# Block-diagonal copies of turned q and k by DMA instead of by three engines, and k turned ahead of q

## The reference

```python
# block 1, for each of 16 batches: N = 128 positions, C = 128, H = 16 heads, HD = 8
mod = silu(c) @ ada_w.T + ada_b                      # shift, scale, gate for both halves
h = layernorm(x) * (1 + scale_msa) + shift_msa
q, k, v = split(h @ qkv_w.T + qkv_b)                 # each 16 heads x 128 x 8
attn = einsum('bhnd,bhmd->bhnm', q, k) * HD ** -0.5
attn = softmax(where(mask, attn, -1e9))
x = x + gate_msa * (einsum('bhnm,bhmd->bhnd', attn, v) @ proj_w.T + proj_b)
x = x + gate_mlp * (gelu(mod(layernorm(x)) @ fc1_w.T + fc1_b) @ fc2_w.T + fc2_b)
```

## Time and profile before

| | |
|---|---|
| time, three runs | 249.68, 250.20, 250.73 us; median 250.2 us |
| span of the profiled execution | 249.0 us (its own device time is not listed apart; the span lies 1.2 us below the median of the runs) |
| busy over the whole span | PE 206.9 us, DVE 186.8, ACT 180.2, POOL 163.5 |
| the 16 steps | about 72.5 to 213 us of the span |
| granted TensorE clock | full in nearly all slices |

### The profile page before, as it was taken

The page is one execution under the profiler, slowest core; times in us unless marked ns, Lnnn a source line. Parts: engine busy times, 40 slices in busy tenths (PEclk is TensorE's granted clock), DMA queues, the critical chain, the costliest instruction groups (busy, mean ns, idle before and its releaser), DMA issues.

```text
span 249.0 us, 5248 instructions
## 1 busy us (share of the span) xinstructions
PE 206.9 (83%) x1596; PEld 154.1 (62%) x1596; DVE 186.8 (75%) x530; ACT 180.2 (72%) x381; POOL 163.5 (66%) x287
## 2 busy tenths in 40 slices
PE   0689998999998687977978787897888778998894
PEld 0548875678876466755746655665666556564784
DVE  0673895647199998989989989989998999058514
ACT  2147769545758788997998988989899877984330
POOL 2499589998676586875876776677689723338500
PEclk9999999999999999999999999999999999999999
DMA  6950000071000000000000000000000000000112
GB/s 159 413 219 0 4 1 0 5 295 42 0 4 0 0 3 1 4 1 0 0 0 0 0 0 0 0 0 0 0 0 3 0 0 3 0 3 0 42 42 86
DMA packets 2768, 8.28 MB, mean 33 GB/s; under 512 B 496, under 2 KB 832, under 8 KB 2496
## 3 DMA queue, kind: packets, MB, share of 16 engines
q1 hardware_dynamic: 2176, 6.22, 6.7%
q10 hardware_dynamic: 576, 1.86, 2.0%
HBM read 7.01 MB, written 1.06 MB: 32 GB/s over the span
## 4 chain that ended last, share of the span: by engine, by line
DVE 34%; PE 31%; issue 19%; ACT 6%; POOL 5%; DMA 2%; DVEq 1%; POOLq 0%; ACTq 0%
PE ps L305 8%; DVE nmax L938 7%; PE ps L295 7%; DVE kdiag L933 7%; DVE nmdiag L956 5%; PE ps L253 3%; DVE xn L781 3%; PE ps L353 2%; PE ps L241 2%; DMA xs<-x 2%; DVE nm L946 2%; PE ps L364 2%; DVE bn_c L979 2%; POOL rstd L1080 2%; DVE qk L923 2%
## 5 line engine op out<-in xcount | busy, mean ns | idle before, releaser
L665 ACT ACTIVATE qdiag<-qxT 32x512 fp32r<-32x512 f32 x64 | 40.2, 628 | 1.4
L938 DVE TENSOR_REDUCE nmax<-ps 128x8 f32<-128x1024 f32 x32 | 37.7, 1217 | 2.2 <-PE ps L353 1.6
L670 ACT ACTIVATE shared<-ps 128x1024 f32<-128x1024 f32 x32 | 31.0, 1021 | 6.6 <-PE ps L377 6.6
L353 PE MATMUL ps<-kdiag,qxT 128*128 128x512 f32 x64 | 20.5, 436 | 16.2 <-DVE kdiag L933 16.2
L1209 POOL TENSOR_TENSOR qkx<-qk,qkx 128x256 fp32r<-128x256 f32 x32 | 22.8, 734 | 16.3 <-ACT qkx L650 16.2
L1214 POOL TENSOR_TENSOR kdiag<-kxT,quarter 128x512 fp32r<-128x512 f32 x16 | 19.9, 1244 | 19.4 <-ACT kxT L659 19.4
L621 ACT ACTIVATE hid<-ps,W 128x512 f32<-128x512 f32 x32 | 21.6, 691 | 14.7 <-PE ps L295 14.6
L933 DVE CAST kdiag<-kxT 32x512 fp32r<-32x512 f32 x48 | 31.2, 651 | 1.0 <-ACT kxT L659 0.6
L305 PE MATMUL ps<-W,hid 128*128 128x128 f32 x256 | 29.9, 275 | 0.0
L305 PEld LDWEIGHTS ps<-W,hid 128*128 128x128 f32 x256 | 29.4, 192 | 0.6 <-issue 0.5
L295 PE MATMUL ps<-hT,W 128*128 128x512 f32 x64 | 29.4, 598 | 0.0
(11 more groups left out here) (148 smaller groups left out, 477.8 us busy)
## 6 DMA issues: line engine op xcount, KB each, us to landing
gate<-gates SPq DMA_DIRECT2D x1, 2048.0 KB, 6.9
xs<-x SPq DMA_DIRECT2D x4, 256.0 KB, 9.4
mask_i<-mask ACTq DMA_DIRECT2D x1, 1024.0 KB, 9.5
W<-weights SPq DMA_DIRECT2D x1, 768.0 KB, 12.0
out<-xs SPq DMA_DIRECT2D x3, 256.0 KB, 2.3
R<-rows ACTq DMA_DIRECT2D x1, 512.0 KB, 7.0
W<-weights SPq DMA_DIRECT2D x1, 512.0 KB, 10.8
W<-weights SPq DMA_DIRECT2D x1, 392.0 KB, 10.1
```

What stands on the lines that cost most here:

```text
L353: ins = mm(ps[:, t, :], qxT[u][:, t], kdiag[u][:, t], start=True, stop=True)
L665: ins = a(qdiag[u][rows, :, r], qxT[u][rows], ACT.Copy)
L670: a(pT[u][:, 2 * e:2 * e + 2], ps[:, 2 * e:2 * e + 2, :].rearrange("n t (r q) -> n t r q", r=4), ACT.Exp, scale=HD ** -0.5).then_inc(s["c_ ...
L938: v.tensor_reduce(nmax[u][:, 8 * e:8 * e + 8], ps[:, 2 * e:2 * e + 2, :].rearrange("n t (r k) -> n (t r) k", r=4), AX.X, ALU.max, negate=T ...
```

## The change

`kdiag` and `qdiag` are filled by DMA. SP, idle before, runs over the 16 batches: it waits until `kxT` of the batch is there, issues four transfers of 32 partitions x 2 KB (64 KB each, on-chip source and destination), waits until `qxT` is there, and issues four more. The semaphores `c_kd` and `c_qd` now count 16 for each transfer, and PE waits for all four. The layout of both tiles becomes (r, t, N) in place of (t, r, N), so that a transfer writes 2 KB in one piece in each partition, and the matmuls read four pieces of 128 columns instead of one of 512. The copies on ACT, DVE and POOL, the tile `quarter` and the semaphore `c_kd3` are gone. k now comes ahead of q everywhere: in DVE's `front_qk`, ACT's `front_hi`, POOL's `lower`, and in PE's and ACT's lists, where `front_k` takes the early place and `front_q` the late one. `front_k` keeps its waits for `c_turn` and `c_v`.

```diff
+            def spread(to, of, b, signal):
+                for r in range(4):
+                    rows = slice(32 * r, 32 * r + 32)
+                    sp.dma_start(to[b % 2][rows, r].bitcast(F32), of[b % 2][rows].bitcast(F32)).then_inc(s[signal], 16)
+
+            sp.wait_ge(s["diag_ok"], 4)
+            for b in range(B):
+                sp.wait_ge(s["c_kT"], b + 1)
+                if b > 1:
+                    sp.wait_ge(s["c_S"], 2 * b - 2)
+                spread(kdiag, kxT, b, "c_kd")
+                sp.wait_ge(s["c_qT"], b + 1)
+                if b > 1:
+                    sp.wait_ge(s["c_ST"], 2 * b - 2)
+                spread(qdiag, qxT, b, "c_qd")
...
             def front_q(b, u):
-                pe.wait_ge(s["c_lo"], 2 * b + 1)
+                pe.wait_ge(s["c_lo"], 2 * b + 2)
...
             def front_k(b, u):
-                pe.wait_ge(s["c_lo"], 2 * b + 2)
+                pe.wait_ge(s["c_lo"], 2 * b + 1)
                 pe.wait_ge(s["c_turn"], b + 1)
                 pe.wait_ge(s["c_v"], b + 1)
...
                     pe.wait_ge(s["c_qT"], b + 1)
-                    pe.wait_ge(s["c_kd"], b + 1)
-                    pe.wait_ge(s["c_kd3"], b + 1)
+                    pe.wait_ge(s["c_kd"], 64 * b + 64)
...
-                    ins = mm(ps[:, t, :], qxT[u][:, t], kdiag[u][:, t], start=True, stop=True)
+                    ins = mm(bank(t), qxT[u][:, t], kdiag[u][:, :, t], start=True, stop=True)
...
-                    pe.wait_ge(s["c_qd"], 3 * b + 3)
+                    pe.wait_ge(s["c_qd"], 64 * b + 64)
...
-                    mm(ps[:, t, :], kxT[u][:, t], qdiag[u][:, t], start=True, stop=False, skip_group_check=True)
+                    mm(bank(t), kxT[u][:, t], qdiag[u][:, :, t], start=True, stop=False, skip_group_check=True)
... PE's step
                 if front:
-                    front_q(b + 1, 1 - u)
+                    front_k(b + 1, 1 - u)
...
                 if front:
-                    pe.wait_ge(s["c_k"], b + 2)
+                    pe.wait_ge(s["c_q"], b + 2)
                 turn_maxima(b, u)
                 scores_t(b, u, 1)
                 if front:
-                    front_k(b + 1, 1 - u)
+                    front_q(b + 1, 1 - u)
... ACT's step
-                front_qdiag(b, u, (1, 2))
                 if end:
                     projected(b - 2, u)
-                front_qdiag(b, u, (3,))
                 if back:
                     back_o(b - 1, 1 - u)
                 if front:
                     front_v(b + 1, 1 - u)
+                    front_k(b + 1, 1 - u)
                     front_q(b + 1, 1 - u)
-                    front_qdiag(b + 1, 1 - u, (0,))
-                    front_k(b + 1, 1 - u)
... DVE's and POOL's steps
-                if front:
-                    front_kdiag(b + 1, 1 - u)
```

More of the change, by code:

```diff
@@ L119, in build @@
         row_mask = sb("row_mask", [128, 1])
-        quarter = sb("quarter", [128, 1])
         row_amp = sb("row_amp", [128, 1])
@@ L186, in build @@
             b_pow b_xn b_xb b_T b_h b_M1 b_gelu b_M2 b_res
-            c_pow c_xb c_gp c_nv c_qbv c_xc c_Tx c_h c_QK c_V c_q c_k c_v c_hiq c_hik c_lo c_Tq c_Tk c_qT c_kT c_qd c_kd c_kd3
+            c_pow c_xb c_gp c_nv c_qbv c_xc c_Tx c_h c_QK c_V c_q c_k c_v c_hiq c_hik c_lo c_Tq c_Tk c_qT c_kT c_qd c_kd
             c_S c_max c_nm c_NT c_nmT c_ST c_exp c_PV c_oT c_T2 c_rden c_on c_T3 c_onT c_pr c_at c_ga c_res c_st
@@ L521, in _ @@
             pe.wait_ge(s["c_h"], 2)
+            pe.wait_ge(s["c_q"], 1)
+            front_k(0, 0)
             front_q(0, 0)
-            front_k(0, 0)
-            pe.wait_ge(s["c_k"], 1)
             front_b(1, 1)
@@ L646, in front_hi @@
             def front_hi(b, u):
-                for n, (ready, slots, signal) in enumerate((("c_q", slice(0, 2), "c_hiq"), ("c_k", slice(0, 4, 2), "c_hik"))):
+                for n, ready, slots, signal in ((1, "c_k", slice(0, 4, 2), "c_hik"), (0, "c_q", slice(0, 2), "c_hiq")):
                     act.wait_ge(s[ready], b + 1)
@@ L659, in front_k @@
                 a(kxT[u][:], bank(7), ACT.Copy).then_inc(s["c_kT"], 1)
[L661 to L666, removed]
             def weights_of(b, u, e):
@@ L716, in _ @@
             a(spare[:], spare[:], ACT.Exp)
+            front_k(0, 0)
             front_q(0, 0)
-            front_k(0, 0)
-            act.wait_ge(s["diag_ok"], 4)
-            front_qdiag(0, 0, (0,))
             step(0, 0, end=False, back=False)
@@ L810, in _ @@
             v.tensor_reduce(sel_f[:], mod32[:, 0:8].rearrange("p (k t) -> p t k", t=4), AX.X, ALU.add)
-            v.tensor_reduce(quarter[:], ident[:, 96:128], AX.X, ALU.add)
             v.tensor_reduce(row_mask[:], mod32[:, MROW:32], AX.X, ALU.add).then_inc(s["mod32_ok"], 1)
@@ L922, in front_qk @@
                 dve.wait_ge(s["c_qbv"], b + 1)
+                v.tensor_tensor(qk[u][:, 1].rearrange("n h d -> n (h d)"), ps[:, 4, C:2 * C], row("qk_b", C, C), ALU.add)\
+                    .then_inc(s["c_k"], 1)
                 v.scalar_tensor_tensor(out=qk[u][:, 0].rearrange("n h d -> n (h d)"), in0=ps[:, 4, 0:C],
@@ L925, in front_qk @@
                     .then_inc(s["c_q"], 1)
[L926 to L934, removed]
             def maxima(b, u, e):
@@ L1026, in _ @@
             front_qk(0, 0)
-            dve.wait_ge(s["diag_ok"], 4)
             b_residual(2)
-            front_kdiag(0, 0)
             front_qk(1, 1)
@@ L1168, in _, with prepare @@
                 p.memset(m[:].bitcast(F32), 0.0).then_inc(s["diag_ok"], 1)
-            def prepare(b, u, end=False, last_kdiag=False):
+            def prepare(b, u, end=False):
                 settled(pool)
@@ L1196, in prepare @@
                 p.tensor_tensor(turn_k[u][:], keep[u][:], one, ALU.add).then_inc(s["c_turn"], 1)
-                if last_kdiag:
-                    front_kdiag(b - 1, 1 - u)
                 if not isinstance(b, int) or b >= 2:
@@ L1204, in lower @@
             def lower(b, u):
-                for n, (hi, lo, signal) in enumerate(((slice(0, 2), slice(2, 4), "c_hiq"),
-                                                      (slice(0, 4, 2), slice(1, 4, 2), "c_hik"))):
+                for n, hi, lo, signal in ((1, slice(0, 4, 2), slice(1, 4, 2), "c_hik"),
+                                          (0, slice(0, 2), slice(2, 4), "c_hiq")):
                     pool.wait_ge(s[signal], b + 1)
@@ L1210, in lower @@
                                     qkx[u][:, n, :, hi], ALU.subtract).then_inc(s["c_lo"], 1)
[L1212 to L1215, removed]
             def residual_1(b, u):
@@ L1232, in step @@
                 if ahead:
-                    prepare(b + 2, u, end, True)
+                    prepare(b + 2, u, end)
                 else:
```

## The result

The changed kernel takes 253.9 us in the median of five runs (253.09 to 259.26), against 250.27 for the kernel before; the ratio is 1.0139 with a 95% interval of 1.0112 to 1.0166. It is slower, by 3.6 us. The likeliest case of the prediction (no change) did not come; its first rival did, the chain through the DMA, near the D of 3.9 for which it gave a period of 9.1 and 255 us. The measured time lies inside the stated range (248 to 260), but in the part that stood there for this rival. A second set of runs of the same kernel gave 253.84 us and 1.0165 (1.0111 to 1.0219).

What follows compares the result with a forecast made beforehand. DVE was taken as the bound before, the loop through ACT and PE after. 13 periods +0.65, step 1 -0.6, jumps +0.75, end -0.6: +0.2 on span 249.0; median 1.2 above: 250.4 us, range 248 to 260.

Steps and rivals of the forecast that it cites:

- The likeliest case of the prediction: Whole kernel: period 8.82 us a step against 8.77, so about no change, 250.4 us; chance 0.43.
- first rival: PE's wait for `c_kd` before the scores becomes the bound from D = 3.6; 255 to 265 us; chance 0.31.
- D: Four `kdiag` issues plus landing of the last: taken as 1.41 + 1.9 = 3.3 us, other side 4.6.
- What bounds the kernel before: DVE runs almost without a gap; PE waits for its `kdiag` copies before the scores, 13.4 us in all.
- What is removed: Per step about 2.0 us of copies on DVE and 2.5 on ACT, leaving 6.3 and 5.4; neither full.
- Loop two: Dependences through the `kdiag` DMA to the next scores: period 5.21 + D, 8.5 us, hidden by 0.3.
- Loop one: Dependences through ACT and PE, from one step's second exponential to the next: 8.79 us, taken as 8.82.
- `qdiag` costed at nothing: `qdiag` transfers on SP land before PE needs them in the next step, with 2.8 us of cover.
- The strided operand at nothing: Matmuls reading four pieces of 128 columns cost nothing, with up to 0.1 us per step as other bound.
- Transfers one after the other: Rival at the four transfers: they serialize, D 7.6, period 12.8, 306 us; chance 0.02.
- The other price of the landing: Skill's price for a 64 KB transfer, 2.15 us; by it D would be 3.56 and the period 8.77.
- Edges: Start and end: step 0 0.4 later but hidden, step 1 gains 0.6, ACT's jumps cost 0.75, end gains 0.6.

Runs made afterwards that it cites:

- the order alone: Kernel before with its copies still on three engines, no DMA, but k ahead of q everywhere: 269.49 us, ratio 1.076 to the kernel before.
- the five issues: Changed kernel plus one more 64 KB transfer, into an unread spare tile, ahead of each batch's four for `kdiag`: 270.96 us, ratio 1.082 to the kernel before.

## Where the prediction was right and where wrong, point by point

- **What bounds the kernel before: right.** DVE, by PE's waits. The run with only `qdiag` by DMA shows that it wasn't ACT: ratio 0.9985 with ACT a fifth less busy. No run freed DVE alone. What I overlooked is that DVE and POOL filled `kdiag` at the same time. In the step of the earlier trace rows two of DVE's three copies take 0.42 us and one 1.17; the 0.65 of the earlier trace rows is a mean. POOL's row of that step:

```profile
158.75 1.27 POOL L1214 TENSOR_TENSOR kdiag<-kxT,quarter 128x512 fp32r<-128x512 f32 x1 [0.83 <-ACT kxT L659]
```

And POOL and DVE in a step of the run of the order alone, one behind the other:

```profile
156.47 1.04 POOL L1214 TENSOR_TENSOR kdiag<-kxT,quarter 128x512 fp32r<-128x512 f32 x1 [0.49 <-ACT kxT L659]
...
157.87 1.34 DVE L933 CAST kdiag<-kxT 32x512 fp32r<-32x512 f32 x3
```

Where the two don't overlap, the same instructions take 1.04 us on POOL instead of 1.27, and 1.26 to 1.35 on DVE instead of 2.03. So about 0.7 us a step of the full engine goes with the overlap. Moving POOL's multiplication alone is a cheaper change that no run tried.

- **What is removed, and that neither engine is full afterwards: right.**
- **Loop two, the start of `front_k`: right.** Counted 3.77 after the scores, measured 3.79. That `front_v` and `back_o` stand ahead of PE's second half is real, and moving v to another bank is worth 0.8 us a step. From there to the first issue 1.24 was counted; it is 1.30 (147.73 to 149.03). The 0.05 for SP's wake had no row behind it; it is 0.02. The last hand-over is 0.12 and not 0.20.
- **Loop two, D: the term that was mis-sized.** The step of the sum was "four issues back to back took 1.87 us, 0.47 each, so the fourth starts 1.41 after the first". It starts 1.81 after the first: behind another issue each takes 0.59, with 0.04 between. The landing, taken as 1.9 from the 128 KB store, is 2.00. D is 3.81 instead of 3.3, and the period 9.02 instead of 8.5. The `mask_rows` row was the cheapest series of issues in the trace of before, and I took it for the price; the three loads of x ahead of it had taken 1.83 us, 0.61 each in the mean (one of them 0.82), and the prediction doesn't weigh them. What made the mask rows cheaper is open: 16 partitions of 2 KB from on chip also took 0.59. Between the two ends that I had kept, 3.3 and 4.6, the chip lies at 3.8, above the 3.6 from which the rival decides. The 3.6 was wrong too: with loop one at 8.35 the rival decides from about 3.1, so that loop two was the bound even at the D that I took.
- **Loop one: also mis-sized, in the other direction.** Counted 8.79 (8.82 with the addition), measured 8.35. Of the 0.44, 0.3 lie in "`front_hi`, `front_h`, `turned_o` as now, 1.50": in the step that I read, `front_hi` waited 0.19 for DVE's q, and `front_h` (at 153.31) stood behind PE's `front_a` (to 153.15), which came late with the scores. Without these waits it is 1.21 from the end of the exponentials to the end of `onT` (156.38 to 157.59), hand-over included. The other 0.15 lie in PE's turn of q, 0.58 in the place where PE had just been idle, and 0.43 in the midst of its list (161.23 to 161.66). I had read a stretch that the old bound was holding up as if it were the bare cost.
- So the forecast of "no change" rests on two errors. With loop one alone put right it would have been 8.5 and a gain; with D alone put right, 9.0 and a loss, which is what came. That 250.4 came out only 1.4% off is luck: loop one, counted too long, took the place of loop two, counted too short. The rival's 9.1 fits because it hangs on loop two only. Its 255 and 265 were counted from the 8.77 of before on top of a sum that already had 8.82, by up to 0.7 us too much.
- **`qdiag` costed at nothing: right.** No wait for it appears among PE's waits, though its issues start 3.8 after the turn of k (156.76 to 160.55) and not 3.1. **The strided operand at nothing: right.** The pair of score matmuls takes 0.72 us as before.
- **Transfers one after the other: this rival falls.** Four issues 0.6 apart each land 2.0 after their own issue; the fifth adds an issue and no landing. The Trainium skill, "DMA: Bandwidth & Descriptors", "Rules for kernel authors", has transfers to disjoint partition halves serialize, and advises one over 128 partitions. In the landing that is not seen here at 64 KB; with 0.6 us between issues, sharing for a shorter time than that couldn't show. One large transfer is cheaper on the queue all the same: an issue of 128 partitions costs 0.61 us, one of 32 costs 0.59.
- **The other price of the landing.** The Trainium skill, "DMA: Bandwidth & Descriptors", "Anatomy of one DMA", has about 2.0 us plus bytes over 436 GB/s, fitted for the other descriptor path, which gives an estimate of 2.15 us for 64 KB. The trace has 2.00, between that and my 1.9. The landing was never the large error: with 2.15 and the 0.47 of an issue the period would have come out at 8.8, and 9.0 was measured.
- **Edges:** step 2 began 1.15 us earlier than before and not 0.6, which hid a part of the loss of the 13 steps.

## What to carry to other kernels

Where a transfer replaces copies on a full engine, the engine's busy time is not the gain: walk the loop of dependences through the transfer, and count every issue on its queue as a serial step of that loop, here 0.6 us each and 2.0 for the last to land. Then shorten that loop rather than the engines: half of the copies back on the engine that has become idle, and the wait ahead of the first issue removed, turned a loss of 1.4% into a gain of 5.3%. Half of the issues on another queue, by itself, gave 2.4%. When a second loop is measured in a trace in which another bound rules, take out the waits that this bound puts into it, or it comes out too long. And where an engine is full, look at its instructions one by one: a mean can hide one that is held up by a neighbour.

## What was not expected of the hardware

DVE and POOL were slower where both filled `kdiag` at once: DVE's three copies took 2.03 us beside POOL's multiplication and 1.26 to 1.35 without it. The rows stand above; that the overlap is the cause is read from them, and no run varied it by itself.

The granted TensorE clock fell where PE idled more. Before, it was full in nearly all slices; with the five issues (about 2 us idle before the scores in each step) it was 0.96 in the mean, with the order alone 0.962, with the DMA in the old order 0.869. In that last run it is seen step by step. Windows of 2 us ahead of the scores at 168.10 and behind them:

```profile
164.00:166.00 2.00, 0.26 (x3) 0.07 (x1) 1.26 (x7) 1.95 (x4) 0.36 (x2) 1.00 0.42 102
166.00:168.00 2.00, 0.00 (x0) 0.00 (x0) 0.00 (x0) 0.00 (x0) 2.00 (x5) 0.91 0.38 94
168.00:170.00 2.00, 1.90 (x5) 1.50 (x6) 0.65 (x1) 0.31 (x1) 0.27 (x1) 0.50 0.00 0
...
172.00:174.00 2.00, 2.00 (x27) 1.58 (x19) 1.25 (x5) 1.29 (x5) 1.61 (x4) 1.00 0.00 0
```

PE was busy 0.26 of 4 us, and then the clock is at 0.50, the level of 1.2 GHz, and full again in the window from 172 us on. A late transfer in the loop can so cost twice, its wait and the slower matmuls behind it. The idle time of a step doesn't settle it alone: with the order alone PE waits about 1.8 us for `vx` in every step, and the clock falls behind every second one. That idle time is what lowers the clock is a reading of these traces; no run varied it by itself.
